# Prologue of a gated cross-attention and ternary feed-forward kernel on one Trainium2 core: later batches' values folded per head from 64 rows, one down-weight piece in another buffer, and the order of the prologue's work rewritten

## What is computed

```python
x = x + tanh(g_xattn[0]) * xattn(layernorm(x), ctx_768, Wq, Wk, Wv, Wo, bo)
x = x + tanh(g_ffn[0]) * ffn(layernorm(x), w_gate, w_up, w_down)

def xattn(x, context, Wq, Wk, Wv, Wo, bo):      # 8 heads of 64
    q, k, v = heads(x @ Wq), heads(context @ Wk), heads(context @ Wv)
    attn = softmax(q @ k.T * 64 ** -0.5)
    return concat(attn @ v) @ Wo + bo

def ffn(x, w_gate, w_up, w_down):               # bitlinear(x, w) = act_quant(x) @ weight_quant(w).T
    h = square(relu(bitlinear(x, w_gate))) * bitlinear(x, w_up)
    return bitlinear(h, w_down)
# act_quant: to 255 levels by each row's largest value
# weight_quant: scale = 1 / clip(mean(abs(w)), 1e-5); q = clip(round(w * scale), -1, 1) / scale
```

## Time and profile before

| | us |
|---|---|
| median of 3 runs (1190.94 to 1191.86) | 1191.34 |
| the profiled execution, whole | 1192.0 |
| its span in the trace | 1190.1 |

### The profile page before, as it was taken

The page is one execution under the profiler, slowest core; times in us unless marked ns, Lnnn a source line. Parts: engine busy times, 40 slices in busy tenths (PEclk is TensorE's granted clock), DMA queues, the critical chain, the costliest instruction groups (busy, mean ns, idle before and its releaser), DMA issues.

```text
span 1190.1 us, 18790 instructions
## 1 busy us (share of the span) xinstructions
PE 1169.0 (98%) x5802; PEld 742.8 (62%) x5867; DVE 1035.5 (87%) x2124; ACT 869.1 (73%) x929; POOL 307.0 (26%) x313
## 2 busy tenths in 40 slices
PE   9989899999999999999999999999999999999998
PEld 7656556666665666666566656656665666666554
DVE  4989898888988888888998888888899888988887
ACT  4877777776886777677877767776787777677764
POOL 3222222222442222222442222222244222222200
PEclk9999999999999999999999999999999999999999
DMA  9792654443444464444444464443443444444333
GB/s 354 263 302 67 156 142 109 98 108 93 101 115 102 114 167 110 97 103 107 101 99 98 114 178 112 98 107 94 101 114 97 104 97 110 96 99 112 84 65 75
DMA packets 286484, 144.69 MB, mean 122 GB/s; under 512 B 254586, under 2 KB 255226, under 8 KB 283889
## 3 DMA queue, kind: packets, MB, share of 16 engines
q1 hardware_dynamic: 286445, 144.32, 47.4%
q10 hardware_dynamic: 4, 0.00, 0.0%
HBM read 57.86 MB, written 24.35 MB: 69 GB/s over the span
## 4 chain that ended last, share of the span: by engine, by line
PE 88%; DVE 4%; DMA 3%; ACT 3%; issue 2%; SPq 0%; POOL 0%; ACTq 0%; DVEq 0%; POOLq 0%
PE gu_ps L1084 34%; PE o_ps L1048 18%; PE y_ps L1098 17%; PE s_ps L66 17%; DMA v_scr<-x 1%; DMA w_down<-in_wu_t 1%; DVE staged L1324 1%; PE gu_ps L1148 1%; DVE half_max L1330 1%; DMA a_scr<-a_spare 1%; DVE w_down L1484 0%; ACT staged L730 0%; ACT x L762 0%; PE y_ps L1141 0%; ACT k_pairs L864 0%
## 5 line engine op out<-in xcount | busy, mean ns | idle before, releaser
L1084 PE MATMUL gu_ps<-w_up,xq_t 128*128 128x512 bf16 x1024 | 241.9, 379 | 0.7 <-DVE staged L1324 0.7
L1084 PE MATMUL gu_ps<-w_gate,xq_t 128*128 128x512 bf16 x951 | 226.3, 379 | 8.6 <-DMA xq_t<-xq 3.9
L1098 PE MATMUL y_ps<-w_down,hq_t 128*128 128x512 bf16 x1008 | 227.8, 379 | 0.0
L1048 PE MATMUL o_ps<-v_sb,pt_high 128*128 128x512 f32 (+1 forms) x640 | 212.8, 413 | 1.1 <-DVE pt_low L1313 1.1
L1324 DVE TENSOR_TENSOR staged<-staged,gu_ps 128x1024 f32<-128x1024 f32 x128 | 155.6, 1215 | 53.8 <-ACT staged L784 53.8
L66 PE MATMUL s_ps<-a_sb,xf_high 128*128 128x308 f32 x1024 | 187.3, 305 | 0.0
L1084 PEld LDWEIGHTS gu_ps<-w_up,xq_t 128*128 128x128 bf16 x1024 | 99.5, 98 | 122.8 <-DVE staged L1324 2.6
L645 POOL TENSOR_TENSOR rstd<-var_eps,neg_half 128x1 f32<-128x1 f32 x128 | 96.6, 755 | 307.9 <-DVE var_eps L1289 275.2
L824 ACT ACTIVATE staged<-staged,h_scale 128x1024 f32<-128x1024 f32 x126 | 137.9, 1141 | 48.7 <-DVE h_scale L1344 48.7
L1098 PEld LDWEIGHTS y_ps<-w_down,hq_t 128*128 128x128 bf16 x1008 | 97.8, 97 | 119.7
L778 ACT ACTIVATE staged<-gu_ps 128x1024 f32<-128x1024 f32 x127 | 128.9, 1015 | 53.9 <-PE gu_ps L1084 53.5
(11 more groups left out here) (146 smaller groups left out, 1439.7 us busy)
## 6 DMA issues: line engine op xcount, KB each, us to landing
xf_sb<-in_x_feat SPq DMA_DIRECT2D x64, 256.0 KB, 2.7
x_sb<-in_x_tok SPq DMA_DIRECT2D x64, 256.0 KB, 2.8
y<-staged SPq DMA_DIRECT2D x63, 256.0 KB, 2.0
staged<-in_wg_t SPq DMA_DIRECT2D x4, 1024.0 KB, 9.8
staged<-in_wd_t SPq DMA_DIRECT2D x4, 1024.0 KB, 7.5
folded<-a_scr SPq DMA_DIRECT2D x3, 1232.0 KB, 5.3
v_scr<-x SPq DMA_DIRECT2D x12, 256.0 KB
folded<-v_scr SPq DMA_DIRECT2D x3, 1024.0 KB, 5.0
```

The costliest lines, as they stand in the source:

```text
L1048: last = nc.tensor.matmul(o_ps[:, :], pt[0:rows, P * c:P * (c + 1)], v_sb[0:rows, v, c, :], start=(c == 0 and pt is pt_high and v == 0), s ...
L1084: last = nc.tensor.matmul(target[:, q, :], xq_t[:, s.par(0), c, :], w[:, c, cols], start=(c == 0), stop=(c == DC - 1))
L1098: last = nc.tensor.matmul(y_ps[:, :], hq_t[:, c, :], w_down[:, c, :], start=(c == 0), stop=(c == FC - 1))
```

## The change

It has five parts.

1. **Values of batches 1 to 3 by head.** `fold_values(b, c)` for b > 0, `place_values(1)` to `place_values(3)`, `take_values` and `store_values` go. In their place `fold_later_values(k)`, k from 0 to 15: head k // 2, and of the 231 keys of batches 1 to 3 the first 116 or the last 115. Each is one product straight from 64 partitions of `v_t` and of `wo_sb`. `take_later_values(k)` evicts it into the same ring of three. Its rows belong to two batches, so `store_later_values(k)` issues two DMAs: of 77 and 39 rows for an even k, of 38 and 77 rows for an odd k, 2 KB a row; `v_scr` is laid out by rows. There are 32 such DMAs where there were 15.
2. **A down piece in the pairs' place.** `load_down(0)` writes to `v_pairs` once batch 0's values are folded, is scaled there, and no longer waits for an up piece.
3. **Loads.** All gate and up pieces are issued in one row behind the first loads, before x and the features of tile 1.
4. **Who does what, and when.** DVE measures five pieces and not four, ACT seven and not eight; DVE scales six and not seven, ACT six and not five. The calls of all five engines stand in a new order.
5. **First steps on DVE.** In step 0 `top_half(0)` goes behind `shift_scores`. Step 1 gets an order of its own, `second_step`.

Core of the diff:

```diff
+def head_part(k):
+
+    h, s = divmod(k, 2)
+    return h, KEYS + FIRST_ROWS * s, FIRST_ROWS - s
+
+
+def part_runs(k):
+
+    _, first, rows = head_part(k)
+    r = 0
+    while r < rows:
+        b, j = divmod(first + r, KEYS)
+        n = min(KEYS - j, rows - r)
+        yield b, j, n, r
+        r += n
...
+            if m == 2 and p == 0:
+                return v_pairs[:, :, :].rearrange("p q n -> p (q n)")[:, 0:PIECE]
...
-                    sp.wait_ge(weight_stage[1][UP_SLOT.index(p)], DONE)
+                    if p == 0:
+                        sp.wait_ge(vo_done, KC)
+                    else:
+                        sp.wait_ge(weight_stage[1][UP_SLOT.index(p)], DONE)
...
+                def store_later_values(k):
+                    at = KEYS * head_part(k)[0]
+                    sp.wait_ge(vo_taken, k + 1)
+                    for b, j, n, r in part_runs(k):
+                        sp.dma_start(v_scr[b, at + j:at + j + n, :],
+                                     v_slots[k % V_OUT_RING][r:r + n, :]).then_inc(v_stored[k % V_OUT_RING], 16)
...
-                load_x(start, 1)
+                load_x(start, 0)
                 load_weight(1, 2, wu_t)
+                load_weight(0, 1, wg_t)
+                load_weight(1, 3, wu_t)
+                load_weight(0, 2, wg_t)
+                load_weight(0, 3, wg_t)
+                load_weight(1, 0, wu_t)
+                load_weight(1, 1, wu_t)
+                store_keys(1, 0)
                 sp.wait_ge(xf_low_done, 1)
                 load_xf(start, 1)
-                load_x(start, 0)
-                load_weight(0, 1, wg_t)
-                load_weight(0, 2, wg_t)
-                load_weight(0, 3, wg_t)
-                load_weight(1, 1, wu_t)
-                store_keys(1, 0)
-                load_weight(1, 3, wu_t)
+                place_bias()
+                load_x(start, 1)
                 load_x(start, 2)
+                load_x(start, 3)
...
+                load_down(1)
+                store_later_values(7)
+                store_keys(2, 3)
+                load_down(2)
+                load_down(3)
...
+                def take_later_values(k):
+                    rows = head_part(k)[2]
+                    act.wait_ge(vo_done, KC + k + 1)
+                    if k >= V_OUT_RING:
+
+                        act.wait_ge(v_stored[k % V_OUT_RING], 32 * (k // V_OUT_RING))
+                    nc.scalar.activation(v_slots[k % V_OUT_RING][0:rows, :], value_slots[(KC + k) % V_RING][0:rows, :], ACT.Copy,
...
+                take_keys(2, 0)
+                take_later_values(4)
                 probs_high(start, 0)
+                high_part(start, 1)
+                take_keys(2, 1)
+                take_later_values(5)
+                take_later_values(6)
+                take_keys(2, 2)
+                scale(1, 3)
+                scale(1, 1)
+                take_later_values(7)
+                take_keys(2, 3)
                 high_part(start, 2)
                 measure(2, 0)
+                take_keys(3, 0)
+                mark_input(start, 0)
+                take_later_values(8)
+                take_later_values(9)
+                take_later_values(10)
+                take_keys(3, 1)
+                exponentials(start, 1)
+                take_later_values(11)
+                take_later_values(12)
+                measure(2, 1)
+                measure(2, 3)
+                part_probs(start, 1)
+                take_keys(3, 2)
+                exponentials(start, 2)
                 high_part(start, 3)
+                take_later_values(13)
+                take_keys(3, 3)
                 join_probs(start, 1)
                 probs_high(start, 1)
+                take_later_values(14)
+                take_later_values(15)
...
+                def fold_later_values(k):
+
+                    h, first, rows = head_part(k)
+                    if k < V_RING:
+
+                        pe.wait_ge(v_split_done, KC + k - V_RING + 1)
+                    else:
+                        pe.wait_ge(vo_taken, k - V_RING + 1)
+                    own = slice(HEAD * (h % 2), HEAD * (h % 2 + 1))
+                    nc.tensor.matmul(value_slots[(KC + k) % V_RING][0:rows, :], v_t[own, h // 2, first:first + rows], wo_sb[own, h // 2, :],
+                                     start=True, stop=True, tile_position=(HEAD * (h % 2), 0)).then_inc(vo_done, 1)
...
                 fold_keys(3, 1)
+                fold_later_values(11)
+                fold_later_values(12)
                 make_scores(start, 2)
                 fold_keys(3, 2)
+                fold_later_values(13)
+                fold_keys(3, 3)
+                fold_later_values(14)
+                fold_later_values(15)
                 total(2)
...
+                def second_step(s):
+                    unmark_hidden(s, -1)
+                    hidden_half(s, 0)
+                    add_attention(s, 1)
+                    input_scale(s, 1)
+                    top_scores(s, 3)
+                    unmark_input(s, 1)
+                    input_stats(s, 3)
+                    hidden_half(s, 1)
+                    shift_scores(s, 3)
+                    top_half(s, 0)
+                    sum_probs(s, 3)
+                    probs_low(s, 2)
+                    hidden_unit_scale(s, 1)
+                    top_half(s, 1)
+                    hidden_scales(s)
...
+                ternary(0, 3, w_gate)
                 dve.wait_ge(rstd1_done, 1)
                 input_stats(start, 1)
+                measure(1, 0)
+                sum_rows(1)
+                ternary(0, 0, w_gate)
+                scale(0, 1)
+                ternary(0, 1, w_gate)
+                ternary(0, 2, w_gate)
+                probs_low(start, 0)
+                find_unit(1)
+                find_hidden_unit()
+                scale(1, 2)
+                scale(1, 0)
+                ternary(1, 3, w_up)
+                ternary(1, 0, w_up)
+                ternary(1, 1, w_up)
+                add_attention(start, 0)
+                input_scale(start, 0)
+                top_scores(start, 1)
+                shift_scores(start, 1)
+                unmark_input(start, 0)
+                ternary(1, 2, w_up)
+                sum_probs(start, 1)
                 dve.wait_ge(rstd1_done, 2)
                 input_stats(start, 2)
+                measure(2, 2)
+                sum_rows(2)
                 top_scores(start, 2)
                 shift_scores(start, 2)
                 dve.wait_ge(units_ready, 1)
                 hidden_unit_scale(start, 0)
                 find_unit(2)
                 find_down_unit()
+                scale(2, 0)
+                sum_probs(start, 2)
                 scale(2, 1)
+                ternary(2, 1, w_down)
+                probs_low(start, 1)
                 ternary(2, 0, w_down)
```

301 lines of the change are left out of this document (108 added, 193 removed).

## The result

| | before | changed |
|---|---|---|
| median of the runs | 1191.14 us | 1199.68 us (1199.28 to 1200.41) |
| ratio | 1 | 1.0068, 95% interval 1.0055 to 1.0080 |
| profiled execution, its span | 1192.0, 1190.1 us | 1200.41, 1198.6 us |
| tile 1's attention starts on PE | 88.8 | 98.1 |
| first gate product of step 3, of step 4 | 139.96, 157.24 | 146.01, 165.02 |

What follows compares the result with a forecast made beforehand. PE bounds the unchanged loop, so only the start of step 3 moves, set by a relay of ACT, PE and DVE: +4.5 at tile 1's attention, -2.7 in the first steps, +1.8 us; median 1193.1, range 1187.6 to 1197.8.

Steps and rivals of the forecast that it cites:

- DVE's start: Prologue: DVE's first measurement behind the keys, on up piece 3, starts at 27.3 instead of 25.96.
- Tile 0's input scale: Prologue milestone on DVE: ready at 68.2, 6.8 us earlier than before.
- the two collisions with POOL: DVE slowed where `low_part` of tiles 1 and 2 runs on POOL: 1.3 us for both, bounds 0 and 2.
- DVE's tail: DVE from the scale to the end of tile 1's `probs_low`, with tile 2's sum: 7.4 us.
- The ring: ACT's evictions 11 and 12 wait for stores of value parts 8 and 9: 2.5 us, bounds 0 and 4.8.
- part 2: From tile 0's input scale to tile 1's attention: 22.6 + 2.5 us, so attention at 93.3, 4.5 later than before.
- Rival A: Slower, chance 0.36: stores land 7.5 us after issue, waits at evictions 11 and 12 cost 4.8, giving 1195.4 us.
- ACT's other waits and work: ACT behind tile 0's input scale: 10.8 us of work and 1.0 of waits for folds.
- PE behind the last key eviction: End of the prologue: PE's last key fold, values 14 and 15, a wait and the sum take 3.4 us.
- at nothing: Effects counted as zero, among them PE's 7 us less of value products, since PE waits for ACT's slots and idles more.
- part 3: First steps: DVE's new order in steps 0 and 1 wins 2.7 us, bounds 1.1 and 3.3.
- part 1: DVE up to tile 0's input scale: from 27.3 to 68.2, 6.8 us earlier than before.

Runs made afterwards that it cites:

- keep_busy: Changed kernel with 24 unread products added on PE where it stands idle, 8 between folds 9 and 10, 16 behind fold 13: 1199.37 us, ratio 1.0058.
- own_rows128: Changed kernel with value parts 11 and 12 in slots of their own and later value products over 128 partitions instead of 64: 1194.35 us, ratio 1.0012.
- own_slots: Changed kernel with value parts 11 and 12 evicted to two slots of their own, waiting for no store: 1195.17 us, ratio 1.0023.
- keys_first: Changed kernel with ACT's last two key evictions and value part 13 ahead of and between its last two measurements: 1199.02 us, ratio 1.0053.
- own_dve_measure: own_slots with down piece 3 measured by DVE instead of ACT and the prologue's end reordered on ACT and DVE: 1194.47 us, ratio 1.0014.
- own_dve_80: own_dve_measure with every value-part store in 80, 48 or 32 rows and the loop's value reloads in 13 loads instead of 2: 1192.97 us, ratio 1.0002.
- down_later: Changed kernel with down piece 3 and tile 3's features loaded behind the stores of value parts 8 to 10: 1199.42 us, ratio 1.0064.
- rows77_48: Changed kernel with only the 38- and 39-row stores written as 48 rows, to places of their own: 1198.66 us, ratio 1.0040.

## Why the prediction was wrong

**Held.** The loop and its 17.28 us. DVE's start (27.3 forecast, 26.96). Tile 0's input scale: 68.2 forecast, 67.3 measured; the two collisions with POOL cost 1.08 and 0.98 (2.30 - 1.22, 1.67 - 0.69), 2.1 where I took 1.3, and what lay beside them was shorter. DVE's tail: 7.4 forecast, 7.5 measured (90.52 to 98.06). The ring waits at evictions 11 and 12, by name. A 64-row fold takes as long as one over 128 rows (two in 1.97 us, two over 128 rows in 1.98 before).

**The step that failed is part 2**, from the input scale to tile 1's attention: 22.6 + 2.5 = 25.1 forecast, 98.1 - 67.3 = 30.8 measured. The 5.7 split like this:

- *The ring, 2.5 forecast, 4.0 measured.* My nearest row was a key store's 5.0 us from issue to landing. That was a median of six, of stores with an even shape. Part 8's took 6.6. The two key stores that the kernel before issued between 65 and 78 show how wide the median was:

```profile
a_scr<-folded SPq DMA_DIRECT2D x1, 308.0 KB, 8.7
a_scr<-a_spare SPq DMA_DIRECT2D x1, 308.0 KB, 4.1
```

The bounds (0 and 4.8) held. Rival A, which "decides from 3.1 us on", had the mechanism right and its price too (4.8); its 1195.4 is too low by the terms below. (Its sentence on the uneven rows adds 1.3 for each such store and gives 1195.5: one makes 1194.4, two 1195.7.)
- *ACT's other waits and work*, 0.7 more than the 11.8 forecast (67.3 to 83.8 is 16.5, less 4.0 and 11.8).
- *PE behind the last key eviction, 3.4 forecast, 6.7 measured.* I wrote that PE's idle time grows and put it "at nothing". It did grow, to 4.47 us in one piece, and the clock fell to half over the folds and the sum that were on the path. I had read 1.00 in every row of the kernel before and took it for a constant. In the relay that cost 2.9 (keep_busy); at step 4 keep_busy and own_rows128 give it 0.3 and 0.9. It is the largest miss of the sum, and the range has no term for it.
- *DVE's tail*, 0.1.

**The second step that failed is the milestone of part 3.** -2.7 forecast, -3.3 measured at step 3, but -1.5 at step 4. The row that says so was in the trace before: 120.95 to 139.96 is 19.01 and not 17.28. A step that begins by waiting for its turned input takes 19.0 itself. I measured the gain ahead of the place where it is given back.

**From the forecast to the result.** The forecast was +1.8, the result +8.5. The 6.7 between them: part 1 -0.9, the ring 1.5, ACT 0.7, PE behind the last key eviction 3.3, DVE's tail 0.1, part 3 1.2, and 0.7 behind step 4. The high ends of the prediction's own terms came to 6.4 over the forecast, 1199.5; the range stopped at 1197.8.

**The sum again, at step 4, by the runs:** ring 5.2 (own_slots, 0.4 of it ahead of the edit), clock 0.9 (own_rows128), and 1.7 left (158.94 against 157.24). The order at the end of the relay is of that size (keys_first won 1.8 with the ring in place, own_dve_measure 2.3 on top of own slots), but no run takes this part alone, so that this last term is argued and not shown. Together 7.8, which is 165.02 - 157.24. These are differences of single executions, of which each can be off by some 1 us for the place of its clock. Of the remaining 0.7 to the 8.5, 0.5 is a wait in the last steps (own_dve_80 has it too, the kernel before does not); 0.2 is open.

DVE shows the same from the other side: from 75 to 90 it works 4.34 us where it worked 11.24, since it waits for ACT (5.16) and PE (5.71). That is an effect of these terms and not a fourth one.

## What to carry to other kernels

A tight relay has no free cover: before putting a longer idle time on an engine "at nothing", ask what else it will lose by standing still. Price a store's landing by its row count and by what stands ahead in the queue, not by the median of another store; 80 and 48 rows instead of 77, 39 and 38 took most of the waits out. Measure a gain behind the first steady step, not at the first milestone it reaches. And before two profiles are compared behind an edit, compare them ahead of it: if the clock fell elsewhere there, their difference is not the edit's.

## What the runs showed of the hardware

- Behind a pause of 4.5 us PE ran at half clock from 81 to 94, through stretches in which it was busy all the time (5.00 of 5.00 from 85 to 90 at 0.50).
- A pause of about the same length did not always go with a fall: 2.1 us at 52 was followed by one at 56 in own_slots and by none in the changed kernel, 1.60 us at 78 by one in own_slots, 1.57 us at 78 by none in the kernel before.
- With stores of 77, 39 and 38 rows what is queued behind them lands late: 7.0 us for the transposing DMA of the input, 3.2 with 80 and 48 rows, 2.5 in own_dve_80.
- Two executions of one kernel differ by 2 us and more at nearly the same mean clock (down_later: 1196.6 at 0.993, 1203.5 at 0.991; rows77_48: 1195.4 at 0.994, 1200.6 at 0.993).
